# First layer: the weighed rows added up on PE inside the next body, and empty second halves left ungathered

## What is computed

```python
rel = edge_emb[edge_type]
h = agg[head]; t = agg[tail]
left = h @ q_w
right = jnp.tanh(rel * t @ k_w)
att = jnp.sum(left * right, axis=1)
e = jnp.exp(att - seg_max[head])
w = e / seg_sum[head]
summed = jax.ops.segment_sum(w[:, None] * rel * t, head, num_segments=n)
agg = summed / jnp.maximum(cnt, 1.0)[:, None]      # then divided by its norm
```

## Time and profile before

| what | value |
|---|---|
| time, median of 3 | 10201.28 us |
| the profiled execution: its time | 10194.69 us |
| its span, first to last instruction | 10192.9 us |
| mean granted TensorE clock | 0.792 of full |
| PE / DVE / ACT / POOL busy | 66% / 76% / 57% / 64% |
| first layer, three hops | about 2040 to 5760 us of the span |
| last layer | about 8760 to 10130 us |

### The profile page before, as it was taken

The page is one execution under the profiler, slowest core; times in us unless marked ns, Lnnn a source line. Parts: engine busy times, 40 slices in busy tenths (PEclk is TensorE's granted clock), DMA queues, the critical chain, the costliest instruction groups (busy, mean ns, idle before and its releaser), DMA issues. The chain is left out here.

```text
span 10192.9 us, 223970 instructions
## 1 busy us (share of the span) xinstructions
PE 6724.1 (66%) x64938; PEld 5458.5 (54%) x64939; DVE 7705.4 (76%) x22255; ACT 5834.0 (57%) x12496; POOL 6563.4 (64%) x5757
## 2 busy tenths in 40 slices
PE   3893986366665666656666478778878876466665
PEld 2882985254554554545555355555555533466664
DVE  9779776477776777767777699989989931677776
ACT  4224226366665666646666389979979920355543
POOL 0777750277776777767777568768858811666665
PEclk8555556578877788877888799999999988777777
DMA  0110115432222322223222212112112264222222
GB/s 23 55 45 15 60 41 197 145 52 53 53 53 44 52 53 53 52 45 52 53 53 53 49 47 59 52 47 59 52 46 59 59 209 162 47 46 46 46 46 44
DMA packets 422026, 630.49 MB, mean 62 GB/s; under 512 B 275527, under 2 KB 332321, under 8 KB 398217
## 3 DMA queue, kind: packets, MB, share of 16 engines
q0 software_dynamic: 192432, 385.10, 18.1%
q1 hardware_dynamic: 162096, 158.87, 5.0%
q10 hardware_dynamic: 67401, 85.32, 2.4%
HBM read 527.43 MB, written 103.02 MB: 62 GB/s over the span
## 5 line engine op out<-in xcount | busy, mean ns | idle before, releaser
L895 POOL DMA_INDIRECT l_land<-table,l_words x3744 | 3598.5, 961 | 1343.2 <-issue 1167.9
L1700 POOL DMA_INDIRECT ell<-gat_stage_pay,gat_stage_at x816 | 1697.1, 2080 | 248.7 <-issue 248.7
L1379 PE MATMUL left_product_ps<-k_w,messageT 128*128 128x128 f32 x5616 | 1035.2, 341 | 529.3 <-ACT messageT L1414 529.3
L1379 PEld LDWEIGHTS left_product_ps<-k_w,messageT 128*128 128x128 f32 x5616 | 872.8, 237 | 734.3 <-ACT messageT L1414 734.3
L2250 PE MATMUL rel_ps<-relation_parts,hot 128*128 128x128 bf16 x11328 | 823.6, 247 | 419.5 <-DVE hot L2349 419.5
L1797 ACT COPY gat_probT<-gat_ps 128x512 f32<-128x512 f32 (+1 forms) x2100 | 1015.3, 551 | 74.8 <-PE gat_ps L1740 66.0
L1373 PE MATMUL left_turned_ps<-ident,message 128*128 128x128 f32 x2808 | 559.1, 334 | 751.5 <-DVE message L1505 751.2
L2250 PEld LDWEIGHTS rel_ps<-relation_parts,hot 128*128 128x128 bf16 x11328 | 803.2, 114 | 441.1 <-DVE hot L2349 441.1
L244 POOL DMA_INDIRECT ell<-pay,position x816 | 841.9, 1032 | 290.4 <-issue 281.2
L1430 ACT ACTIVATE weighed<-kept,l_prob 128x128 f32 x2784 | 888.9, 391 | 59.1 <-ACT l_prob L961 58.9
L1373 PEld LDWEIGHTS left_turned_ps<-ident,message 128*128 128x128 f32 x2808 | 385.8, 173 | 853.9 <-DVE message L1505 850.7
(11 more groups left out here) (332 smaller groups left out, 15746.0 us busy)
## 6 DMA issues: line engine op xcount, KB each, us to landing
gcn_edges<-counts SPq DMA_DIRECT2D x50, 1600.0 KB, 8.1
l_land<-table,l_words POOLq DMA_INDIRECT x3744
rows<-low_dram SPq DMA_DIRECT2D x34, 1536.0 KB
counts<-pair_turned_sb ACTq DMA_DIRECT2D x12, 3200.0 KB, 9.4
logs<-pair_logs ACTq DMA_DIRECT2D x12, 3200.0 KB, 18.2
ell<-pay,position POOLq DMA_INDIRECT x816
ell<-gat_stage_pay,gat_stage_at POOLq DMA_INDIRECT x816
l_words<-ell SPq DMA_DIRECT2D x476, 8.0 KB
```

The costliest lines, as they stand in the source:

```text
L895: pool.indirect_dma_start(self.land[:, p, s, :], None, table[:, :], bass.IndirectOffsetOnAxis(ap=self.words[:, p, s, 0:1], axis=0)).then_i ...
L1379: mm = pe.matmul(right_ps[:, k * H + j, :], messageT[:, k, j, :], k_w[:, :], start=True, stop=True)
L1700: pool.indirect_dma_start(c.ells[1][:, :], bass.IndirectOffsetOnAxis(ap=stage_at[n % 2][:, t:t + 1], axis=0), stage_pay[n % 2][:, t, :], N ...
```

## The change

Three parts. **(1)** In the first layer the reduction of the 8 weighed rows leaves DVE: PE adds them with 8 accumulating fp32 matmuls by the identity (`add_up`), between half 0 and half 1 of its next iteration, and DVE folds the result into `total` with one fused operation (`add_sum`). **(2)** DVE's order changes: the products with `left_now` come ahead of `add_body`. **(3)** POOL no longer gathers second halves that hold only absent edges, nor the 117th body, in the first and the last layer; SP walks the blocks' plan to know them, and in the first layer POOL holds the 25 plan words in registers and its loop is written out once for each block (`gather_by_plan`). `open` clears the buffer of the second halves.

```diff
 def open(self, v):
+        self.nc.vector.memset(self.land[:, :, H:S, :], 0.0)
+        v.drain()
...
 feed(sp), one step for each body n:
+        self.by_parity(sp, n, first_half)            # stand on rows_in[p][0]; rows_ready[0] += 1
+        self.pass_words(sp, base + n + 1)
+        with sp.If(has_second):
+            self.by_parity(sp, sp.snap(s), ...)       # stand on rows_in[q][1]
+        sp.sem_inc(self.rows_ready[1], 1)
+        self.by_parity(sp, n, lambda p: go_on(n, p))
 and after the last body:
+        for h in range(HALVES):
+            sp.sem_inc(self.rows_ready[h], 1)
...
+    def gather_by_plan(self, pool, hop, bodies, table, words):
+        for b, word in enumerate(words):
...
+            with pool.Fori(0, many) as i:
+                n = pool.snap(first + i)
+                def both(p):
+                    stand(pool, self.turns, self.words_ready, hop * (bodies + 2) + n + 1)
+                    stand(pool, self.turns, self.rows_used[0], hop * bodies + n + 1)
+                    half(p, 0, self.rows_in[p][0])
+                    with pool.If(i < whole):
+                        stand(pool, self.turns, self.rows_used[1], hop * bodies + n + 1)
+                        self.by_parity(pool, pool.snap(s0 + i), lambda q: half(p, 1, self.rows_in[q][1]))
+                self.by_parity(pool, n, both)
...
+    def add_sum(self, v, total, weighed_sum, sum_ready, n, sum_used):
+        v.wait_ge(self.prob_ready, n)
+        V.tensor_copy(self.top_now[:, :], self.top_new[:, :])
+        V.tensor_reduce(self.part[:, :], self.prob[:, :, :].rearrange("p s h -> p h s"), AX.X, ALU.add)
+        v.drain()
+        V.scalar_tensor_tensor(out=self.denom[:, :], in0=self.denom[:, :], scalar=self.keep[:, 0:1], in1=self.part[:, :],
+                               op0=ALU.mult, op1=ALU.add)
+        v.wait_ge(sum_ready, n)
+        V.scalar_tensor_tensor(out=total[:, :], in0=total[:, :], scalar=self.keep[:, 0:1], in1=weighed_sum[:, :],
+                               op0=ALU.mult, op1=ALU.add).then_inc(sum_used, 1)
...
+                def add_up(w):
+                    pe.wait_ge(sum_used, w + 1)
+                    for k in range(HALVES):
+                        pe.wait_ge(weighed_ready[k], w + 1)
+                    for s in range(S):
+                        mm = pe.matmul(sum_ps[:, :], c.ident[:, :], weighed[:, s, :], start=(s == 0), stop=(s == S - 1))
+                    mm.then_inc(sum_ready, 1)
...
-                    with pe.Fori(0, all_bodies) as i:
+                    with pe.Fori(1, all_bodies) as i:
                         turn_kinds(m + i + 2)
-                        for k in range(HALVES):
-                            rights(n + i + 1, k)
-                            relations(m + i + 2, k)
+                        rights(n + i + 1, 0)
+                        relations(m + i + 2, 0)
+                        add_up(hop * all_bodies + i + (-1))
+                        rights(n + i + 1, 1)
+                        relations(m + i + 2, 1)
+                    add_up(hop * all_bodies + all_bodies + (-1))
...
                 def add_body(n):
-                    for k in range(HALVES):
-                        v.wait_ge(weighed_ready[k], n)
-                    soft.add(v, weighed, total, part, D)
+                    soft.add_sum(v, total, sum_ps, sum_ready, n, sum_used)
...
                             soft.mark(c.iota_row)
+                            v.drain()
+                            v.wait_ge(soft.score_free, a0 + i + 1)
+                            (the products of right and left_now, moved up to here)
                             with v.If(body > 0):
                                 add_body(a0 + i)
                             (finish_block and the clearing, as before)
                             v.drain()
                             soft.scores(v)
                             messages(body + 1, n + 1, m + 1, 1)
```

More of the change, by code:

```diff
@@ L849, in of_parity, with each_body, by_parity @@
         return (bodies + (1 - p)) >> 1
[L851 to L856, removed]
+    def each_body(self, eng, visit):
+        with eng.Fori(0, self.z.blocks) as b:
+            many, whole, first = self.block(eng, b)
+            seconds = self.second(eng, b)
+            with eng.Fori(0, many) as i:
+                visit(eng.snap((first + i).with_bounds(min_val=0, max_val=self.z.bodies - 1)), i < whole, seconds + i)
+    def by_parity(self, eng, n, visit):
+        with eng.If((n & 1) < 1):
+            visit(0)
+        with eng.If((n & 1) > 0):
+            visit(1)
     def load_words(self, sp, body, p):
@@ L871, in feed, with go_on @@
         self.load_words(sp, 1, 1)
[L873 to L879, removed]
+        def go_on(n, p):
             if kinds_done:
@@ L885, in feed @@
+        self.each_body(sp, step)
+        for h in range(HALVES):
+            sp.sem_inc(self.rows_ready[h], 1)
+        self.pass_words(sp, base + bodies)
+        last = sp.snap(bodies + (-1))
+        self.by_parity(sp, last, lambda p: go_on(last, p))
         self.pass_words(sp, base + bodies + 1)
     def gather_all(self, pool, hop, bodies, table):
[L889 to L897, removed]
@@ new lines, in gather_all, with read_plan, half, both @@
+        self.each_body(pool, step)
+    def read_plan(self, pool):
+        return [pool.value_load(self.plan[0:1, b:b + 1], min_val=1, max_val=(1 << 31) - 1)
+                for b in range(self.z.blocks)]
+    def gather_by_plan(self, pool, hop, bodies, table, words):
+        most = self.z.bodies
+        def half(p, h, landed):
+            for s in range(h * H, (h + 1) * H):
+                pool.indirect_dma_start(
+                    self.land[:, p, s, :], None, table[:, :],
+                    bass.IndirectOffsetOnAxis(ap=self.words[:, p, s, 0:1], axis=0)).then_inc(landed, 16)
+        seconds = hop * self.all_second(pool)
+        for b, word in enumerate(words):
+            halves = word & ((1 << HALF_BITS) - 1)
+            many = pool.snap(((halves + 1) >> 1).with_bounds(min_val=1, max_val=most))
+            whole = pool.snap((halves >> 1).with_bounds(min_val=0, max_val=most))
+            first = pool.snap((word >> HALF_BITS).with_bounds(min_val=0, max_val=most))
+            s0 = pool.snap(seconds)
+            with pool.Fori(0, many) as i:
+                n = pool.snap(first + i)
+                def both(p):
+                    stand(pool, self.turns, self.words_ready, hop * (bodies + 2) + n + 1)
+                    stand(pool, self.turns, self.rows_used[0], hop * bodies + n + 1)
+                    half(p, 0, self.rows_in[p][0])
+                    with pool.If(i < whole):
+                        stand(pool, self.turns, self.rows_used[1], hop * bodies + n + 1)
+                        self.by_parity(pool, pool.snap(s0 + i), lambda q: half(p, 1, self.rows_in[q][1]))
+                self.by_parity(pool, n, both)
+            seconds = s0 + whole
@@ L1343, in _ @@
                     stand(pool, stream.turns, stream.table_in, hop * z.stored + z.stored)
[L1344 removed]
+                    stream.gather_by_plan(pool, hop, pool.snap(all_bodies + 1), c.table, words)
             @block.tensor
@@ L1405, in _ @@
                 act.sem_inc(hotT_moved, 1)
+                act.sem_inc(soft.score_free, 1)
                 def move_kinds(m):
```

48 lines of the change are left out of this document (38 added, 10 removed).

## The result

The changed kernel takes 11216.45 us (median of 4 runs, 11195.59 to 11221.89), the kernel before beside it 10200.62 us: ratio 1.0993, 95% interval 1.0977 to 1.1009. It is slower by 10%. The forecast was 11110 us in a range of 10480 to 11310. The profiled execution has a span of 11219.9 us.

A forecast was written before the change was run, and what follows sets the result against it. POOL's gathers were taken as the bound, 10.19 us a body; a serial chain of 8.0 - 0.16 + 2.45 + 2.23 + 0.33, together 12.85 us, adds 915 us over three hops to 10194.7, plus 2: about 11110 us, range 10480 to 11310.

The forecast's parts named there:

- The bound before: First layer's hops: POOL gathers without a stop, 10.19 us a body, 8 gathers of 0.96 + 0.31 us.
- The chain: First layer: PE's sum and DVE's steps form one serial chain from message to message, 12.85 us a body against 10.19.
- Relations of half 0 at the clock of the stretch: PE's work up to the end of `relations` of half 0: 6.59 us at the high clock, 8.0 taken.
- M: The end of DVE's `messages` half 1, from which the prediction counted the times of a body.
- The add-up: PE's 8 fp32 matmuls, 16 operations, behind `relations` of half 0: 2.45 us, less 0.16 of overlap.
- The quarter at the low clock: Share of PE's add-up taken at the low clock: 2.05 + 0.4 = 2.45 us.
- DVE afterwards: DVE from the ready sum to the next end of `messages`, fused operation of 0.29 us included: 2.23 us.
- The end of a block: `finish_block` and the clearing on DVE, between sum and scores: 1.54 us in 25 of 116 bodies, 0.33 a body.
- 13 + 4 us a hop: First layer, if POOL bounds: 13 us from the empty second halves, 4 from the 117th body.
- Rival 1: More PE work keeps its clock high in the first layer: 11.04 us a body, 10480 us; chance 0.15 for 10480 to 10800.
- Rival 2: The sum is there in time and POOL still bounds, so only fewer gathers count: 10145 us; chance 0.07.
- Rivals 3 and 4: POOL's gathers come off whole, 76 us a hop, 9970, chance 0.02; gains and chain cancel within 0.2%, chance 0.03.

The follow-up runs named there:

- e3: The changed kernel with the add-up moved to the head of PE's turn, ahead of the transposes of kinds; 10175.92 us, ratio 0.9978.
- e10: e2 with SP passing the words of body n+1 before it stands for the first half of body n; 10220.96 us, ratio 0.9975.
- e2: The kernel before with only the empty second halves and the 117th body left out of POOL's gathers; 10198.25 us, ratio 0.9995.
- e12: The changed kernel with one of the sum's 8 matmuls, 7 of 8 weighed rows missing from the sum; 10844.75 us, ratio 1.0586.
- e11: The changed kernel with the sum's 8 matmuls done twice; 12020.09 us, ratio 1.1732.
- e9: e3 with SP passing the words of body n+1 before it stands for the first half of body n; 10082.25 us, ratio 0.9842.
- e5: The changed kernel with the add-up behind the transposes of kinds, ahead of `rights` of half 0, on the slow chip; 13806.69 us, ratio 1.0560.
- e8: The changed kernel with one of the sum's 8 matmuls, run on the slow chip; 13848.99 us, ratio 1.0587.
- e7: The changed kernel with the sum's 8 matmuls done twice, run on the slow chip; 14893.4 us, ratio 1.1386.

## Why the prediction was right

**The bound before: right, but half of it.** POOL at 10.19 us a body was read rightly, and e3 shows it again once the chain is short. That the chain of before was as long, so that nothing is to be had from POOL alone, the prediction didn't see (e10).

**The chain: right, and it is the mechanism.** DVE waits for the sum in 81 of 82 bodies, and moving the add-up by three places takes 1040 us off (e3). The 10.71 us that the prediction read off for a body wholly at the high clock is met too: the first body shown, from 2698.48 to 2710.98, takes 12.50 us with a block's end of 1.71, 10.8 without it. By terms, 13.05 us against the 12.85 of the prediction:

- *Relations of half 0 at the clock of the stretch*: 8.0 us taken. The rest of the body leaves 13.05 - 1.9 - 2.34 - 0.37 = 8.4. In the body at the high clock it was M + 6.67 (M is 1.65 us ahead of the group at 2700.13), as predicted; in the low one shown above it ends at 2721.30, M + 10.3, well above the M + 7.95 of the half low body that stood for it. This is the term that was too small.
- *The add-up*: 2.45 less 0.16 taken, 1.8 (2705.15 to 2706.93) to 2.0 measured; its operations have a mean of 283 ns, so they nearly all run at the high clock. The quarter at the low clock was too much, by 0.4. This and the term above are off by 0.4 us each and cancel, and that is luck.
- *DVE afterwards*: 2.23 taken; 2723.33 to 2725.67 is 2.34. The fused operation takes 0.35 us instead of 0.29, and behind the row maximum DVE pauses 0.20 us in each of the 348 bodies, which it didn't before.
- *The end of a block*: 1.54 us taken, 2707.41 to 2709.12 is 1.71, 0.37 instead of 0.33 a body.

Over all 348 bodies the hops grew by 2.90 us a body, where 2.63 was forecast: 94 of the 106 us by which 11110 falls short. The rest lies in the last layer (1376.5 us from its first to its last `comp`, against 1371.4, the +5 of the range) and in the spread of the runs.

**Part 3: that it brings nothing beside the chain holds, the price behind it doesn't.** "13 + 4 us a hop" was given for the case that POOL bounds. e2 is that case and shows 3.9 and 2.4 us by the starts of the hops' first gathers (1256.8 and 1257.0 us apart instead of 1260.7 and 1259.4): about the 117th body's 4.2 us and nothing for the 13 halves. Two things were wrong. The new waiting at a left-out half was put at 2 to 2.7 us and is 3 to 5, with 1 to 2 more behind some. And DVE and PE had little room for what early words give back: in e10 they take off 12.6 us in three hops. Whether the 4 us of the 117th body came off in the changed kernel too isn't shown.

**Rival 1 (the high clock): out.** The clock in the hops stayed at 0.80 with 16 more operations in each body. The Trainium skill ("TensorE: Matmul & The Clock Gate", "What's actually happening") says that the throttled state is the default and that activity releases it. The traces agree in part: e12 leaves 14 operations out, and the clock falls to 0.74. But the sum of activity doesn't tell the level. From 2080 to 3150 us PE is busy 773 us in e11 at a clock of 0.80 and 765 us in e3 at 0.93, and 683 us in e12 at 0.74 and 680 in the kernel before at 0.81. What differs between the changed kernel and e3 in the timelines is how long PE stands in one piece before it goes on: 4.10 us ahead of the low groups at 2712.63, at most 1.78 us in e3 between 2700 and 2730, where all groups run high. That isn't the whole of it either: PE stands for DVE's message 2.7 us a body in the changed kernel, in e11 and in e12 alike (223, 187 and 246 us over 82, 70 and 90 bodies), and the operations of `left_product_ps` take 355, 388 and 386 ns. What sets the level here stays open.

```profile
2080.00:3150.00 1070.00, 764.84 (x5936) 671.41 (x5936) 609.92 (x3379) 676.72 (x1802) 762.35 (x797) 0.93 0.22 50
```

**Rival 2 (in time, POOL bounds)** is false of the change and true of e3: the turning point "the chain must be under 10.2 us" was met by another place in PE's order, not by faster operations, but its 10145 counted 56 us off for the gathers, and e3 gave 25. **Rivals 3 and 4** didn't come: even e9, with POOL's stands cut to 27 us a hop, stays above 9970 us.

## What to carry to other kernels

When work moves to another engine, ask first which point of that engine's order it takes and what must run ahead of it; the same 16 operations cost 1040 us more in the middle of PE's turn than at its head, where the kernel is as fast as before. An engine with 2 us of idle time a body and a consumer that needs the result before its next step form a ring: add up the ring from one message to the next, at both levels of the clock, and compare it with the bound of today. And where two limits lie close together, test their removal together: here each alone gave at most 0.25%, both 1.6%.

## What the runs showed of the hardware

- The same program on the same inputs takes 10200.9 us on one chip, 10244.5 on a second and 13073.8 on a third. On the third, in the trace of e5, DVE, ACT and POOL have operations of the same length as elsewhere, and ACT and DVE begin many of them 4 to 9 us after what they need. Times from two such chips can't be compared, and a change's ratio can differ as well: e8 and e12, one kernel, agree with 1.0587 and 1.0586, e7 and e11, one kernel, don't, with 1.1386 and 1.1732.
- Two kernels with the same PE operations (the changed one and e3) run at a clock of 0.80 and 0.93. In e3, where PE's idle times are shorter, the operations of `left_product_ps` take 305 ns against 355. That the one makes the other isn't shown.
- In e2 52 gathers fewer in the first hop, 66 us of POOL's work, came back as 60 us of new stands, 3 to 5 us at a left-out half. With SP's words passed earlier (e9 against e3) 40 us of such stands went.
